# Attention-side x is turned by VectorE, out of a pass through DRAM on ScalarE's queue, instead of by TensorE; slot sums, x copies and key turns change their places

## The reference

```
x = q                                   # (8, 512, 256), 4096 tokens of 256
xn = layernorm(x)
attn: s = xn @ k.T                      # k: 1024 x 256, each batch of 512 tokens
      s *= scale                        # four rows of xn (every 128th), flattened to 1024 columns
      softmax(s) @ v
ffn:  shared = gelu(xn @ Wfc_s + b) @ Wproj_s + b      # hidden 1024
      top 2 of 8 experts by softmax(xn @ Wr), gates normalised over the two
      routed = sum over the two of gate * (gelu(xn @ Wfc[e] + b) @ Wproj[e] + b)
out = x + attn + shared + routed
```

## Time and profile before

| | |
|---|---|
| median of 3 runs | 772.53 us |
| the profiled execution, its own time | 771.95 us |
| its span | 770.4 us |
| granted TensorE clock, mean | 0.998 |
| PE busy, share of the span | 754.9 us, 98% |
| DVE, ACT, POOL busy | 470.0, 448.6, 231.7 us (61%, 58%, 30%) |

### The profile page before, as it was taken

One profiled execution on the slowest core, in us unless ns is written; L12 is line 12 of the kernel. 1 busy time (PEld: TensorE's weight loads), 2 busy tenths in 40 slices (PEclk: granted clock), 3 DMA queues, 4 the chain that ended last, 5 costly groups with the idle time before them and its releaser, 6 DMA issues.

```text
span 770.4 us, 21336 instructions
## 1 busy us (share of the span) xinstructions
PE 754.9 (98%) x6937; PEld 643.6 (84%) x6937; DVE 470.0 (61%) x1162; ACT 448.6 (58%) x862; POOL 231.7 (30%) x272
## 2 busy tenths in 40 slices
PE   6999999999999999999999999999999999999998
PEld 5798876777777777999899988888888888888887
DVE  5878858888887797454544544444344444336776
ACT  5567447666668775465556555555544555544452
POOL 2445426656566752022112121221221221210000
PEclk9999999999999999999999999999999999999999
DMA  9547222657575958654533567546465646304564
GB/s 314 198 167 178 98 83 83 225 189 244 194 229 183 348 199 286 179 168 132 162 69 69 163 154 223 174 124 212 123 185 157 178 133 202 97 29 148 161 205 151
DMA packets 109949, 131.29 MB, mean 170 GB/s; under 512 B 64496, under 2 KB 91472, under 8 KB 103488
## 3 DMA queue, kind: packets, MB, share of 16 engines
q1 hardware_dynamic: 84784, 108.30, 46.0%
q0 software_dynamic: 6480, 17.77, 6.2%
q10 hardware_dynamic: 18624, 4.46, 2.8%
HBM read 89.32 MB, written 41.18 MB: 169 GB/s over the span
## 4 chain that ended last, share of the span: by engine, by line
PE 87%; DVE 5%; issue 2%; DMA 2%; ACT 1%; POOL 1%; SPq 1%; DVEq 0%; POOLq 0%; ACTq 0%
PE ps_v L1399 32%; PE ps_h L1379 31%; PE ps_v L1532 10%; PE ps_h L1468 10%; PE ps_t L1482 3%; DMA slots_x<-x_split,pos_i 1%; DVE h_split L1008 1%; ACT h L804 1%; DMA x_split<-slots_x 1%; POOL slots_x L712 0%; DVE x_t L920 0%; DMA prob<-k_pass 0%; PE ps_v L1406 0%; PE ps_v L1330 0%; DVE acc L1016 0%
## 5 line engine op out<-in xcount | busy, mean ns | idle before, releaser
L1008 DVE TENSOR_TENSOR h_split<-h,h_split 128x512 f16<-128x512 f32 (+1 forms) x224 | 142.4, 642 | 160.2 <-ACT h_split L810 159.8
L804 ACT ACTIVATE h<-ps_h,b_fc 128x256 f32<-128x256 f32 (+1 forms) x320 | 125.9, 444 | 156.2 <-PE ps_h L1379 156.2
L1379 PE MATMUL ps_h<-x_t,w_split 128*128 128x256 f16 (+1 forms) x1920 | 193.3, 261 | 0.7 <-DVE x_t L1209 0.6
L1399 PE MATMUL ps_v<-w_stage,h_split 128*128 128x256 f16 x1704 | 192.6, 273 | 0.1
L1379 PEld LDWEIGHTS ps_h<-x_t,w_split 128*128 128x128 f16 x1920 | 170.3, 98 | 18.2 <-DVE x_t L1209 0.8
L1399 PEld LDWEIGHTS ps_v<-w_stage,h_split 128*128 128x128 f16 x1704 | 166.3, 98 | 19.4 <-issue 0.3
L748 POOL DMA_INDIRECT tokens_y<-prob,to_i x71 | 74.1, 1044 | 325.5 <-DMA tokens_y<-prob,to_i 194.1
L810 ACT CAST h_split<-h 128x512 f16<-128x512 f32 (+1 forms) x224 | 130.8, 584 | 10.0
L1532 PE MATMUL ps_v<-v_split,p_t 128*128 128x256 f16 x768 | 88.8, 272 | 0.0
L804 ACT ACTIVATE h<-ps_h,b_t 128x256 f32<-128x256 f32 x128 | 53.4, 468 | 60.8 <-PE ps_h L1379 58.8
L1468 PE MATMUL ps_h<-k_t,x_t 128*128 128x512 f16 x384 | 88.1, 379 | 0.0
(11 more groups left out here) (157 smaller groups left out, 595.9 us busy)
## 6 DMA issues: line engine op xcount, KB each, us to landing
w_split<-wpack SPq DMA_DIRECT2D x17, 1024.0 KB, 5.7
w_stage<-wpack SPq DMA_DIRECT2D x17, 1024.0 KB, 5.3
wpack<-w_split SPq DMA_DIRECT2D x8, 1024.0 KB, 5.0
wpack<-h_split SPq DMA_DIRECT2D x8, 1024.0 KB, 5.0
y_rows<-tokens_y SPq DMA_DIRECT2D x32, 256.0 KB, 3.2
b_pj<-bias_e SPq DMA_DIRECT2D x40, 128.5 KB
w_stage<-in_L_ffn_Wfc_dram SPq DMA_DIRECT2D x4, 1024.0 KB, 7.6
scale_b<-key_scale SPq DMA_DIRECT2D x8, 512.0 KB, 8.0
```

The source lines that it names most:

```text
L804: ins = nc.scalar.activation(h32[:, hc, 0:n], ps_h[:, hc * TILE:hc * TILE + n], ACT.Gelu_apprx_tanh, bias=bias[:, hc:hc + 1], scale=1.0 / WS)
L1008: ve.tensor_tensor(h_split[par][:, 1, 2 * b:2 * b + 2, 0:n], h32[:, 2 * b:2 * b + 2, 0:n], h_split[par][:, 0, 2 * b:2 * b + 2, 0:n], ALU.s ...
L1379: ins = mm(ps_h[:, hc * TILE:hc * TILE + cols], wv[:, wl, c, hc * P:(hc + 1) * P], x[:, xl * DC + c, 0:cols], start=n == 0, stop=n == 3 * ...
L1399: ins = mm(ps_y[a][:, :], h_split[par][:, xl, c, a * P:(a + 1) * P], wv[:, wl, c, :], start=n == 0, stop=n == 3 * HC - 1)
```

## The change

x of the tiles 9 to 15 is no longer turned by TensorE. ScalarE's queue stores `x_split` of the tile to a DRAM buffer `x_pass` (256 KB, behind the exponential of phase 1) and loads it back in four quads (64 KB each, behind the probabilities' copy of phase 2) into the memory of `xn`; before the loads ScalarE waits for the store's landing. VectorE turns it in phase 0 of the next three query tiles, behind the lo part of the probabilities. The router product comes after the values of its query tile, as do rank and the count. The small routing operations go to the beginning of VectorE's next query tile, the lo part of x goes before the scaled scores, the tables' first two pieces come a query tile later. In stage 1, VectorE's tile has the first slot sums and the copy of x before the last lo part, and the key turns at its end.

```diff
+            def store_pass(i):
+                par = i % 2
+                if passed(i) > 1:
+                    wait_ge(act, s_pass_in[par], 16 * QUADS * (passed(i) - 1))
+                wait_ge(act, s_hl, 2 * i)
+                act.dma_start(rows(x_pass, par * TILE, TILE), x_split[i % 3][:, :, 0:ROW]).then_inc(s_pass_out[par], 16)
+
+            def load_pass(i):
+                par = i % 2
+                wait_ge(act, s_row_out[par], 16 * (i // 2 + 1))
+                wait_ge(act, s_pass_out[par], 16 * passed(i))
+                for qd in range(QUADS):
+                    src = x_pass[par * TILE:(par + 1) * TILE, qd * QW:(qd + 1) * QW].rearrange("(b t) f -> t b f", t=32)
+                    act.dma_start(xn_quad[par][qd * 32:(qd + 1) * 32, :, :], src).then_inc(s_pass_in[par], 16)
...
             for u in range(QT):
                 p_hi(u)
+                if u % 3 == 2 and NA + 1 + u // 3 < SHARED:
+                    load_pass(NA + 1 + u // 3)
...
                     nc.scalar.activation(gap_exp[:, :], gap_all[:, :], ACT.Exp, scale=1.0 / WS).then_inc(s_gexp, 1)
+                if u % 3 == 1 and NA + 1 + u // 3 < SHARED:
+                    store_pass(NA + 1 + u // 3)
...
                 front_b(split=i + 1)
+                split_h(i, i % 2, banks=(2,))
+                slots_first(i)
+                copy_xt(i + 1)
+                split_h(i, i % 2, banks=(3,))
+                evict_shared(i - 1, i - 1, part=0)
+                slots_rest(i)
+                evict_shared(i - 1, i - 1, part=1)
                 if i >= 4:
                     turn_keys(i - 4)
-                split_h(i, i % 2, banks=(2, 3))
-                evict_shared(i - 1, i - 1, part=0)
-                copy_xt(i + 1)
-                front_b(route=i)
-                evict_shared(i - 1, i - 1, part=1)
...
+            def turn_pass(i):
+                par = i % 2
+                dve.wait_ge(s_pass_in[par], 16 * QUADS * passed(i))
+                ve.transpose(x_t[:, i, :, :].rearrange("p c (b t) -> p b c t", t=32),
+                             xn_quad[par].rearrange("p b (r c) -> p b c r", r=32)).then_inc(s_xt, 1)
+
             for u in range(QT):
                 k, phase = u // 3, u % 3
                 i = NA + 1 + k
+                if phase == 1 and i - 1 < SHARED:
+                    front_a(route=i - 1, bank=side[(u - 1) % 2])
+                if phase == 2 and i - 1 < SHARED:
+                    front_b(route=i - 1, bank=side[(u - 1) % 2])
+                if u == 24:
+                    tables(u)
                 if u >= 2:
                     finish(u - 2)
                 p_lo(u)
+                if phase == 0 and k and i - 1 < SHARED:
+                    turn_pass(i - 1)
+                if phase == 1 and i < SHARED:
+                    front_b(split=i)
                 if u + 2 < QT:
                     scale_scores(u + 2)
                 if phase == 0 and i < SHARED:
                     front_b(norm=i)
-                if phase == 1 and i < SHARED:
-                    front_b(split=i)
-                if phase == 0 and i - 1 < SHARED:
-                    front_a(route=i - 1, bank=side[u % 2])
-                if phase == 1 and i - 1 < SHARED:
-                    front_b(route=i - 1, bank=side[u % 2])
-                if phase == 2 and i < SHARED:
-                    copy_xt(i, bank=side16[u % 2])
...
-            def tr1_side(i, u):
-                pe.wait_ge(s_hl, 2 * i)
-                pe.wait_ge(s_fin, u - 1)
-                transpose_quads(x_split[i % 3], out=side16[u % 2]).then_inc(s_tr, 1)
...
-                side_work(u)
                 if u:
                     values(u - 1)
+                side_work(u)
```

## The result

The kernel after takes 813.96 us (median of 4 runs, 808.15 to 815.35), the kernel before beside it 772.54 (771.46 to 772.57). The ratio is 1.0528 [1.0512, 1.0543]: 41.4 us slower. Forecast were 780.2 us and 768 to 792. The sign and the place are as forecast, the size is five times too small. The profiled execution took 814.31 us, its span is 812.7, its mean granted clock 0.977.

A forecast was written before the change was run, and what follows sets the result against it. TensorE bounds the kernel, but in attention a 20.2 us cycle of latencies would set the pace. Profiled 771.95 + 0.4 (first stage) + 7.9 (attention) - 0.6 (hand-over) = 779.6, as median 780.2 us; range 768 to 792.

The forecast's parts named there:

- The bound and the mechanism: Whole kernel: TensorE carries 87% of the chain; in attention, a closed chain of latencies through DRAM would set the pace.
- A ring over the pass: Attention: from one VectorE turn of x to the next, 20.2 us against 18.58 TensorE needs; +7.9 us in all.
- the landing of the store and of the loads: Attention: store lands in 3.1 us (2.9 to 5); loads 5.2 us after issue (3.7 to 7.0), just covered.
- The 1.9 us for query tile 20: Attention, last cycle: 1.9 us more, since ScalarE has both parts of a weight job behind the load there.
- The first router of the ring: Attention, tile 9: TensorE reaches this router product at 135.3 us, the turn done at about 135.1, so no wait.
- Contended transfers: Attention: beside SP's megabyte transfers, loads land in 7.0 us, cycle 21.9 us, first router waits; 792 us, chance 0.13.
- The four issues: Attention, ScalarE: four loads at 0.34 us each and some 0.1 between them, 1.8 us a cycle.
- GpSimd's hold of the lo part: Attention, VectorE: the lo part of x waits 1.05 us for GpSimd's split, plus 0.65 of its own: 1.7 us.
- ScalarE's sequencer runs ahead: Attention: the store goes out as the exponential starts, not after it; 0.1 us.
- Stage 1: Shared expert: waits removed -1.6, tile 6 +0.2, last key turn before the first scores +1.8; sum +0.4 us.
- The hand-over: Before the routed steps: tables done about 1.6 us sooner, the 0.6 us wait of the first routed product goes; -0.6.
- TensorE's turns are dearer: Attention, rival: turns cost 390 ns each, not the row's 0.055 us; 21.8 us freed, about 750 us; chance 0.01.

The follow-up runs named there:

- experiment 1: Changed kernel with SP's weight transfers of the attention stage cut to a sixteenth and wpack's rest filled with zeros at the hand-over; 853.42 us, filling included.
- experiment 4: Changed kernel with its attention part alone, the first stage ordered as in the kernel before; 815.89 us, 41.2 over before.
- 8: Changed kernel with load behind the exponential, VectorE's turn and router two query tiles later, key turns in mid tile; 777.78 us, ratio 1.0040 to the kernel before.
- experiment 10: Changed kernel with load behind the exponential, VectorE's turn and router two query tiles later, first stage as before; 775.44 us, ratio 1.0044 to the kernel before.
- Experiment 9: Kernel before, TensorE still turning x, with only side work behind the values, routing steps and tables' first pieces later; 771.80 us, ratio 0.9996.

## Why the prediction was wrong, point by point

- **The bound and the mechanism** were right. A ring over the pass sets the pace, TensorE waits before the router products, and the rest of the kernel is unchanged (from the first routed product to the end 469.0 us, 469.2 before).
- **The step that failed is the landing of the store and of the loads**, two terms of the ring's sum that were sized too small: "Landing: 512 KB of the same 1 KB rows took 3.1 us", and "the loads land 5.2 us after issue (3.7 to 7.0), which the 4.85 us ... just cover". Measured: 3.0 to 8.2 for the store (median 4.9), 9.5 to 10.8 for the last load in three of seven cycles. The 3.1 came from a stretch where SP moves no weights, the 5.2 from the routed stage. Both rows were real and of the wrong stretch. The stretch itself had a row for it: the 1 MB weight loads, which in the kernel before land in 7.1 to 10.9 us between 140 and 300 us. In the kernel after, the pass's slow transfers end within 0.2 to 0.7 us of the last large one of SP's. The prediction named the sign itself, "the turn waiting for its load long after the lo part (then landings rule, not ScalarE's order)"; three of the seven turns do.
- **In us**: the six rings took 151.2 where 121.2 + 1.9 was forecast, 28.1 more. The 1.9 us for query tile 20 came as forecast and are in the 151.2: from the first load's issue to the turn the last cycle took 8.6 us (280.99 to 289.59), the one before it with hidden loads 6.9 (230.16 to 237.09). The first router of the ring stood at 139.75 instead of 135.3 (+4.4: stage 1 was 2.4 later, the rest is that router's wait of 2.06, where none was forecast). 28.1 + 4.4 = 32.5, and 258.6 + 32.5 = 291.1, where query tile 22 starts at 291.19 (250.72 before).
- **Contended transfers**, the rival at 0.13, was the true case, and at 792 it was too low. It let the loads land in 7.0 and left the store at 3.1. What a cycle sees is one of the two, store or loads, 5 us late; that both places are exposed, so that shifting the pair only moves the hit, was not seen.
- **The four issues** took 1.9 to 3.2 us instead of 1.8: under load each of ScalarE's own issues lasts longer (median 474 ns, up to 1382). In experiment 1 they took 1.81 to 1.85.
- **GpSimd's hold of the lo part** came nearly as taken: "the wait, 1.05 us, plus 0.65". The answer on that line, 113 to 300 us:

```profile
L1004 DVE TENSOR_TENSOR x_split<-xn,x_split x7: 692/1457/1529, 124.3 to 269.8; 128x512 f16<-128x512 f32 x7
```

  Median 1457 ns, a mean of 704 before, and six of the seven took 1.1 us or more (the one of 692 ns is the first). That is up to 0.8 us more, where 1.05 was forecast. The forecast leaned on the Trainium skill's rule (SBUF — State Buffer, Who interferes with whom), that an operation of VectorE with two SBUF inputs contends with one of GpSimd that reads SBUF. The trace agrees: at 193.52 the lo part took 1.52 us, while GpSimd was splitting from 192.36 to 194.49.
- **ScalarE's sequencer runs ahead**: the store was issued 0.10 us after the exponential began (196.51 and 196.41), as forecast.
- **Stage 1** was forecast at +0.4. In the kernel after, the waits of tiles 1, 4 and 6 are gone and the first scores wait 1.72 us (forecast 1.8). But TensorE's turn at 88.76 now waits 1.15 us for the lo part of x, where the forecast had only +0.2 for tile 6, and the one at 29.46 waits 2.13 instead of 1.06, of which the forecast said nothing (experiment 4, with the old order, shows 2.14 there, so this is not the new order's alone). So the first turn of the probabilities came at 115.41 and not at 113.04, 2.4 us later. By itself the part costs 3.9 us, with the key turn in the middle some 2; under the ring it cannot be seen (experiment 4), nor between 8 and 10. The first stage also differs from one execution to the next: in experiment 4, with the order of before, query tile 0's turns of the probabilities stood at 116.82 us, against 113.04 (beside it the kernel before took 2.2 us longer too). Its true price stays open.
- **The hand-over**, -0.6: the wait is gone (343.73, without one), but from query tile 22 to there it took 52.5 us and not 49.9, since after the wait of 5.40 us at 290.97 the clock stood at 0.52 (291 to 297 us): turns of the probabilities 1.95 us instead of 1.04 and scores 4.65 instead of 2.75, 2.8 us together.
- **TensorE's turns are dearer**, rejected: rightly. Without them three query tiles take 18.65 us instead of 19.02, so eight turns cost 0.37 us, no more than their row says.

Not tried was a kernel in which SP's full pairs are issued at moments that touch neither store nor loads; experiment 1 makes them small instead of moving them. Nor was one tried with the scales' loads made small.

No version was found that beats the kernel before. Experiment 9 equals it.

## What to carry to other kernels

A ring of latencies is paid in full at each round, whatever slack its engines have; sum it from one use to the next, and price each transfer in it by what lands in the same stretch, beside the same neighbours, not by its own size. If a pass through DRAM must be made, first give its consumer room (the load's later place took away 10 of the 41 us, two query tiles of room another 28), and let no engine wait for a landing on whose next work the main chain stands. Half a microsecond of TensorE's time a round is not worth such a ring.

## What was not expected of the hardware

- A store of 256 KB took 2.2 us to land when SP moved little, 3.0 to 3.7 between the 1 MB pairs, and 6.8 to 8.2 issued 1.5 to 2 us behind one; the last of four 64 KB loads issued together with a pair took 9.5 to 10.8, otherwise 1.9 to 3.1.
- Issuing a DMA itself becomes slower beside them, 0.31 to 1.38 us each on ScalarE.
- After the wait of 5.40 us TensorE ran some 6 us at its lower level, after the one of 1.82 us (188.07) not at all; in a kernel held by a ring of transfers this cost next to nothing (0.2 us of 25), although it is up to 2.8 us of TensorE's time a wait. In experiment 10, without the ring, it cost 1.7 us behind one wait.
